# Linear attention and MLP: gamma folded into weights and biases, residual sums taken from PSUM, values copied by ScalarE

## The reference, cut to what matters

```
xn   = rmsnorm(h, scale1)                       # h * scale1 * (sqrt(128) + 1e-6) / norm(h)
q, k, v = xn @ qkv_w.T                          # 16 heads of 8
q, k = exp(-0.5 q^2), exp(-0.5 k^2)
kv   = sum over rows of k (x) v                 # per sequence and head
out  = (q @ kv) / (q @ sum(k) + 1e-6)
h1   = h + gamma * (out @ proj_w.T + proj_b)
hdd  = gelu(rmsnorm(h1, scale2) @ conv1_w.T + conv1_b)      # 256 wide
x    = x + h1 + gamma * (hdd @ conv2_w.T + conv2_b)
```

## Time and profile before

| what | value |
|---|---|
| median of 3 runs | 1204.99 us (1204.27 to 1205.66) |
| the profiled execution | 1205.75 us, of which the span of instructions is 1203.9 us |
| linear stage, 311.7 to 372.2 us | 60.5 us |
| MLP stage, 372.2 to 404.6 us | 32.4 us |
| busy share of the span | PE 86%, DVE 63%, ACT 46%, POOL 37% |

### The profile page before, as it was taken

The page is one execution under the profiler, slowest core; times in us unless marked ns, Lnnn a source line. Parts: engine busy times, 40 slices in busy tenths (PEclk is TensorE's granted clock), DMA queues, the critical chain, the costliest instruction groups (busy, mean ns, idle before and its releaser), DMA issues. The chain is left out here.

```text
span 1203.9 us, 30164 instructions
## 1 busy us (share of the span) xinstructions
PE 1036.5 (86%) x12369; PEld 782.5 (65%) x12369; DVE 753.6 (63%) x1475; ACT 549.6 (46%) x1000; POOL 447.1 (37%) x496
## 2 busy tenths in 40 slices
PE   5899999998576679999999989997889958699992
PEld 4788888886454557777777756665436625567771
DVE  2455655554495568888888858886568778631222
ACT  2455555554233246666666635553545424342220
POOL 1132333322245624444444433321324157236142
PEclk9999999999898769999999979997989869889996
DMA  8300050000000100000000000000784110011324
GB/s 246 127 1 1 2 142 2 1 1 1 0 1 1 36 1 2 3 3 3 2 3 2 2 1 2 2 2 2 228 323 124 30 36 3 3 57 55 97 91 126
DMA packets 37943, 53.15 MB, mean 44 GB/s; under 512 B 3024, under 2 KB 29264, under 8 KB 37424
## 3 DMA queue, kind: packets, MB, share of 16 engines
q1 hardware_dynamic: 35824, 46.97, 12.4%
q0 software_dynamic: 1984, 4.26, 1.0%
HBM read 29.08 MB, written 22.14 MB: 43 GB/s over the span
## 5 line engine op out<-in xcount | busy, mean ns | idle before, releaser
L1515 ACT COPY e_PT<-probsT 128x512 f32<-128x512 f32 x192 | 103.5, 589 | 154.8 <-PE probsT L1363 154.8
L1363 PE MATMUL probsT<-W,e_P 128*128 128x128 f32 x768 | 106.8, 284 | 15.5 <-ACT e_P L1522 15.5
L505 POOL TENSOR_TENSOR c_P<-c_P,c_rl 128x1024 f32<-128x1024 f32 x32 | 60.7, 1896 | 127.7 <-DVE c_rl L645 127.7
L1522 ACT ACTIVATE e_P<-e_P 128x1024 f32<-128x1024 f32 x96 | 102.7, 1070 | 5.6 <-DVE e_P L1620 4.0
L1363 PEld LDWEIGHTS probsT<-W,e_P 128*128 128x128 f32 x768 | 86.8, 144 | 19.1 <-ACT e_P L1522 17.7
L1617 DVE TENSOR_REDUCE e_mx<-scores 128x16 f32<-128x1024 f32 x64 | 78.4, 1225 | 30.6 <-PE scores L1351 29.3
L642 DVE TENSOR_REDUCE c_rl<-c_P 128x8 f32<-128x1024 f32 x32 | 39.0, 1220 | 81.9 <-ACT c_P L329 81.9
L542 PEld LDWEIGHTS misc<-c_xs,c_AQ 128*128 128x128 f32 x488 | 62.2, 194 | 35.0 <-issue 33.4
L1190 POOL TENSOR_TENSOR e_RK<-e_Ks,W 128x512 f32<-128x512 f32 x64 | 65.9, 1039 | 51.2 <-PE scores L1351 28.3
L1620 DVE TENSOR_TENSOR e_P<-scores,e_mx 128x1024 f32<-128x1024 f32 x64 | 78.4, 1225 | 6.5
L1376 PEld LDWEIGHTS mixed<-e_Vbd,e_PT 128*64 128x64 f32 x2048 | 64.9, 138 | 26.1 <-issue 19.3
(11 more groups left out here) (366 smaller groups left out, 2345.7 us busy)
## 6 DMA issues: line engine op xcount, KB each, us to landing
hbm_dist<-u_Z SPq DMA_DIRECT2D x16, 768.0 KB, 8.4
u_S<-hbm_dist SPq DMA_DIRECT2D x64, 128.0 KB, 2.8
e_w<-in_w SPq DMA_DIRECT2D x12, 256.0 KB, 2.8
W<-in_wpack SPq DMA_DIRECT2D x1, 2489.0 KB, 13.1
hbm_slots<-c_blank SPq DMA_DIRECT2D x6, 350.0 KB, 6.2
e_xin<-hbm_slots SPq DMA_DIRECT2D x6, 350.0 KB, 3.4
W<-in_wpack SPq DMA_DIRECT2D x1, 2048.0 KB, 8.7
hbm_results<-c_blank SPq DMA_DIRECT2D x1, 2048.0 KB, 11.5
```

What stands on the lines that cost most here:

```text
L505: pool.tensor_tensor(pr, pr, bc(rl[:, a.up, :].unsqueeze(2), [P, PAIRS, KEYS]), ALU.mult).then_inc(s["scaled"], 1)
L1363: last = pe.transpose(K.psT[:, i * P:(i + 1) * P], Pr[:, n % 2, i * P:(i + 1) * P], K.ident)
L1515: act.copy(PT[:, n % 2, half * 512:(half + 1) * 512], K.psT[:, half * 512:(half + 1) * 512]).then_inc(s["tcopied"], 1)
L1522: act.activation(Pr[:, n % 2, :], Pr[:, n % 2, :], ACT.Exp, scale=0.5 if n < TOTAL else CSCALE).then_inc(s["exped"], 1)
```

## The change

The products with gamma leave the loops. Four operations at the start of `stage_linear` make `projG = projT * gamma`, `projB = proj_b * gamma`, `downB = conv2_b * gamma` and `downG = conv2T * gamma`. PE multiplies by `projG` and `K.downG`, so PSUM already holds gamma times the product. POOL adds the two bias rows to `Xmid` and to `X` in the linear stage, right after a group's `scales`; in the MLP stage it adds `Xmid` to `X` one step earlier than before. DVE, which copied PSUM plus bias into `ya`, now adds PSUM straight into `Xmid` (line 782 of the changed kernel) or `X`; the buffers `ya` are gone. The copy of the values goes from DVE to ACT, and the two masked columns of a tile are made by one operation in place of two.

```diff
@@ stage_linear, DVE
+                def scaled_weights():
+                    gamma = row("gamma")
+                    dve.tensor_tensor(projG[:, :], w("projT"), gamma, ALU.mult).then_inc(s["weights"], 1)
+                    dve.tensor_tensor(projB[:, :], row("proj_b"), gamma, ALU.mult).then_inc(s["weights"], 1)
+                    dve.tensor_tensor(downB[:, :], row("conv2_b"), gamma, ALU.mult).then_inc(s["weights"], 1)
+                    dve.tensor_tensor(K.downG[:, :, :], w("conv2T").rearrange("p (c d) -> p c d", c=2),
+                                      bc(gamma.unsqueeze(1), [P, 2, D]), ALU.mult)
...
-                        for b in range(TB):
-                            last = dve.tensor_scalar(KV[:, a.par, i, b, D:], w("headmask"),
-                                                     ps[:, TB * D + b:TB * D + b + 1], None, ALU.mult)
+                        last = dve.tensor_tensor(KV[:, a.par, i, :, D:], bc(w("headmask").unsqueeze(1), [P, TB, HEADS]),
+                                                 bc(ps[:, TB * D:TB * D + TB].unsqueeze(2), [P, TB, HEADS]), ALU.mult)
...
-                def bias(a):
+                def mid(a):
...
                     dve.wait_ge(s["y"], a.n + 1)
-                    wait(dve, s["xm"], a.n - 1)
-                    dve.tensor_tensor(ya[:, a.par, :, :], pY[:, 0:N].rearrange("p (i d) -> p i d", i=G),
-                                      bc(row("proj_b").unsqueeze(1), [P, G, D]), ALU.add).then_inc(s["ya"], 1)
+                    dve.wait_ge(s["xb"], 2 * (a.n + 1))
+                    xl = K.Xmid[:, a.n * G:(a.n + 1) * G, :]
+                    dve.tensor_tensor(xl, pY[:, 0:N].rearrange("p (i d) -> p i d", i=G), xl, ALU.add).then_inc(s["ya"], 1)
...
                 first = At(0, 0, 1)
                 stats(first)
                 stats(first.plus(1))
+                scaled_weights()
                 xnorm(first)
@@ stage_linear, POOL
-                def mid(a):
+                def biases(a):
...
-                    pool.wait_ge(s["ya"], a.n + 1)
-                    y = ya[:, a.par, :, :]
-                    pool.tensor_tensor(y, y, bc(row("gamma").unsqueeze(1), [P, G, D]), ALU.mult).then_inc(s["yg"], 1)
-                    pool.wait_ge(s["yg"], a.n + 1)
-                    xl = K.Xmid[:, bass.ds(a.n * G, G), :]
-                    pool.tensor_tensor(xl, xl, y, ALU.add).then_inc(s["xm"], 1)
+                    pool.wait_ge(s["xn"], a.n + 1)
+                    for x, v in ((K.Xmid, projB), (K.X, downB)):
+                        xl = x[:, a.n * G:(a.n + 1) * G, :]
+                        pool.tensor_tensor(xl, xl, bc(v[:, :].unsqueeze(1), [P, G, D]), ALU.add).then_inc(s["xb"], 1)
@@ stage_linear, ACT (phi)
-                    act.wait_ge(s["v"], a.n + 1)
+                    act.wait_ge(s["kv"], a.n + 1)
+                    wait(act, s["KV"], a.n - 1)
+                    for b in range(TB):
+                        last = act.copy(vb[64 * b:64 * b + 64, a.par, :, b * D:(b + 1) * D],
+                                        pKV[64 * b:64 * b + 64, :].rearrange("p (i c) -> p i c", i=G)[:, :, D:])
+                    last.then_inc(s["v"], 1)
@@ stage_mlp, DVE (bias becomes result, in the same place of the step)
-                    wait(dve, s["ym"], a.n - 1)
-                    dve.tensor_tensor(ya[:, a.par, :, :], pY[a.par][:, 0:N].rearrange("p (i d) -> p i d", i=G),
-                                      bc(row("conv2_b").unsqueeze(1), [P, G, D]), ALU.add).then_inc(s["ya"], 1)
+                    dve.wait_ge(s["xsum"], a.n + 1)
+                    xl = K.X[:, a.n * G:(a.n + 1) * G, :]
+                    dve.tensor_tensor(xl, pY[a.par][:, 0:N].rearrange("p (i d) -> p i d", i=G), xl, ALU.add).then_inc(s["ya"], 1)
@@ stage_mlp, POOL (residual)
-                    pool.wait_ge(s["ya"], a.n + 1)
...
+                    xl, ml = K.X[:, a.n * G:(a.n + 1) * G, :], K.Xmid[:, a.n * G:(a.n + 1) * G, :]
+                    pool.tensor_tensor(xl, xl, ml, ALU.add).then_inc(s["xsum"], 1)
```

More of the change, by code:

```diff
@@ L681, in stage_linear @@
     K.Xmid = K.early.enter_context(nc.sbuf_tensor("Xmid", [P, TILES, D], F32))
+    K.downG = K.early.enter_context(nc.sbuf_tensor("downG", [P, 2, D], F32))
     with ExitStack() as st:
         s = K.sems(st, "l2_", "weights chain var scaled rs xn turned xnT q kv squared phi v kvm KV num rden rdenok o oT oTc y "
-                              "ya yg xm")
+                              "ya xb")
         sb = lambda n, sh, dt=F32: st.enter_context(nc.sbuf_tensor("l2_" + n, sh, dt))
-        Wqkv = sb("Wqkv", [D, 3 * D])
+        Wqkv, projG = sb("Wqkv", [D, 3 * D]), sb("projG", [D, D])
+        projB, downB = sb("projB", [P, D]), sb("downB", [P, D])
         st6, mv = sb("st6", [P, 2, G, 6]), sb("mv", [P, 2, G, 2])
@@ L788, in step @@
                     xnorm(a.plus(1))
-                    values(a)
                     stats(a.plus(2))
                     divide(a.plus(-1))
-                    bias(a.plus(-2))
+                    mid(a.plus(-2))
                 first = At(0, 0, 1)
@@ L831, in _ @@
                 scales(first.plus(1))
-                run_units(pool, 1, GROUPS, step, 2)
+                pool.wait_ge(s["weights"], 6)
+                run_units(pool, 1, GROUPS, step, 0)
             @block.scalar
@@ L871, in _ @@
                 xT(At(0, 0, 1))
+                act.wait_ge(s["weights"], 3)
                 run_units(act, 1, GROUPS, step, 2)
@@ L946, in step @@
                     proj(a.plus(-2))
-                pe.wait_ge(s["weights"], 3)
                 turn(At(0, 0, 1))
+                pe.wait_ge(s["weights"], 4)
                 run_units(pe, 1, GROUPS, step, 2)
@@ L994, in xnorm, with result @@
                     last.then_inc(s["xn"], 1)
-                def bias(a):
+                def result(a):
                     if not inside(a):
@@ L1006, in step @@
                     squares(a.plus(2))
-                    bias(a.plus(-1))
+                    result(a.plus(-1))
                 first = At(0, 0, 1)
@@ L1028, in residual @@
                         return
-                    pool.wait_ge(s["ya"], a.n + 1)
-                    y = ya[:, a.par, :, :]
-                    at = bass.ds(a.n * G, G)
-                    pool.tensor_tensor(y, y, bc(row("gamma").unsqueeze(1), [P, G, D]), ALU.mult).then_inc(s["yg"], 1)
-                    pool.tensor_tensor(K.X[:, at, :], K.X[:, at, :], K.Xmid[:, at, :], ALU.add).then_inc(s["yg"], 1)
-                    pool.wait_ge(s["yg"], 2 * a.n + 2)
-                    pool.tensor_tensor(K.X[:, at, :], K.X[:, at, :], y, ALU.add).then_inc(s["ym"], 1)
+                    xl, ml = K.X[:, a.n * G:(a.n + 1) * G, :], K.Xmid[:, a.n * G:(a.n + 1) * G, :]
+                    pool.tensor_tensor(xl, xl, ml, ALU.add).then_inc(s["xsum"], 1)
                 def step(a):
                     scales(a.plus(2))
-                    residual(a.plus(-1))
+                    residual(a)
                 first = At(0, 0, 1)
@@ L1097, in down @@
                             last = pe.matmul(pY[a.par][:, i * D:(i + 1) * D], hT[:, a.par, c, i * P:(i + 1) * P],
-                                             w("conv2T", c * P, P), start=(c == 0), stop=(c == 1))
+                                             K.downG[:, c, :], start=(c == 0), stop=(c == 1))
                     last.then_inc(s["y"], 1)
```

19 lines of the change are left out of this document (4 added, 15 removed).

## The result

The changed kernel takes 1187.15 us (median of 6 runs, 1186.93 to 1191.66) against 1205.92 us (median of 6, 1204.27 to 1206.57) of the kernel before. In two later sessions, on two chips, the changed kernel had 1189.99 us against 1205.38, ratio 0.9867 (0.984 to 0.9894), and 1190.19 against 1205.36, ratio 0.9883 (0.9837 to 0.9929). So the gain is real in every session, but both kernels scatter much more than the three runs shown before let me think.

What follows compares the result with a forecast made beforehand. Chains between engines, with no engine full, were taken to bound both stages. Gains of 5.2 + 0.4 + 1.6 + 1.8 + 2.8, less 0.1 for weights, gave 11.7 us: 1204.99 to 1193.3 us, range 1190.5 to 1197.0.

Steps and rivals of the forecast that it cites:

- The period, 5.2 us: Linear stage: time per group falls from 5.97 to 5.13 us, a gain of 5.2 us from first to last sums.
- M: Linear stage: time of the new masking on DVE, forecast 1.08 us against 1.70, with bounds 1.24 and 0.95.
- the path over PE: Linear stage: masking, normalising, hop, then PE's transposes to sums at 1.72 us, and 1.17 to masking; 5.13 us a group.
- The path over ACT, 4.67: Linear stage: chain from sums through qkv products, ACT's copies and exponentials, 4.67 us; shorter than PE's, 0.46 to spare.
- The last masking and the stage's end on VectorE, 0.4 + 1.6: Linear stage's end: the last masking gains 0.4 us; ending with DVE and not POOL gains 1.6.
- The scaled weights, -0.1: Linear stage's start: four products with gamma fit where DVE idles for POOL's first scale; they cost nothing or 0.1 us.
- The MLP stage, 1.8 + 2.8: MLP stage: all eight groups run at 2.59 us, gaining 1.8; ending with DVE and not POOL gains 2.8.
- the term for the clock: MLP stage: the clock's rise can come a little sooner or later, about one more us of spread.
- a rival in which it changes at one place: Attention stage's entry: 2.4 GHz is kept where the clock was 1.2 GHz, worth 6.9 us, total 1186.4; chance 7%.
- Rival 1: Linear stage: POOL's two new additions fall on DVE's normalising, margin 0.17 us; costs 5.7 us, total 1199.0; chance 9%.
- my own list: Signs of being wrong: DVE's normalising starts inside a POOL addition, sums wait for ACT, or the attention stage's clock differs.
- Rivals 2, 4 and 5: MLP loop stays with DVE and POOL, 1194.7, 8%; low clock lasts longer, 1207.4, 3%; nothing arrives, 1205, 3%.

Runs made afterwards that it cites:

- after again: The changed kernel profiled a second time, nothing edited against the changed kernel; the profiled execution took 1187.21 us.

## Why the prediction was wrong, by its own steps

**The mechanisms held, and so did their sum, in part by luck.** 11.7 us were forecast; the two stages give 12.0 us between the first two profiles and 12.3 between the two with equal later stages, and 11.6 are left at equal clock over all runs. In the first pair the linear stage gave 1.6 more than its 7.2 and the MLP stage 1.4 less than its 4.6, and the two errors nearly cancel. Term by term:

- *The period, 5.2 us.* Measured 6.5: the first and the last sums (first pieces) are 325.14 and 358.55, so 33.4 us against 39.9. The period is 4.66, not 5.13. M was 0.87, not 1.08, below its bound of 0.95: a joined masking takes 0.18 us but the next operation starts 0.09 to 0.10 behind it, and I had taken 0.20 from start to start out of the row of 0.19. And the rest of the turn was 3.79, not 4.05, in all three kernels in which the sums no longer wait for ACT (this one and the experiments with the copies alone and with two masks). I had subtracted the wait of 0.22 from the path over PE, but the wait had cost more: it also kept the sums' weights from being loaded ahead. The load's own row in the kernel before shows 0.41 us, not 0.22:

```profile
340.71 0.30 PEld L893 LDWEIGHTS scores<-l_vb,l_phk 128*128 128x128 f32 x2 [0.41 <-ACT l_phk L864]
```

  From the transposes to the sums there were 1.94 us before and 1.56 after, 0.38 less. With the wait, load and product start together (340.71 here, 335.93 with the masks alone) and the first two products take 0.70 us; without it, the load starts 0.11 us sooner (334.55 and 334.66 in "after again") and they take 0.60. Against that, the collision at the end took 0.83 back, which I had as a rival and not as a term.
- *The path over ACT, 4.67, as the shorter one.* It is shorter than 4.67: from the sums (334.53) the last exponential ends 4.50 us later (339.03), and PE starts the next sums 0.16 after that. So some 0.16 us are to spare, where I counted 0.46.
- *The last masking and the stage's end on VectorE, 0.4 + 1.6.* From the last sums to the next stage 8.64 us before (363.63 to 372.27), 6.46 after: 2.2.
- *The scaled weights, -0.1.* Nothing. The rule from the Trainium skill ("SBUF — State Buffer", "Who interferes with whom"), by which they could cost 1.04 us, did not show in these rows: four operations with two SBUF inputs ran beside POOL's root at 0.26 to 0.41 us. With POOL's 128x256 additions the rule does agree in the kernel before: VectorE's squares in the MLP stage, which read one tile as both inputs, took 0.80 us beside such an addition (389.31) and 0.28 free. Normalising, with one such input, was held by them as well.
- *The MLP stage, 1.8 + 2.8.* 3.2 in the first pair of profiles, 4.6 in the second. In the first, 0.9 was lost because the second product came 10.4 us after the stage's start against 9.5 before, its rows still at the 1.2 GHz level, and 0.4 in the gap to the next stage.

**The step that failed is the term for the clock, and with it the range.** I gave the clock "about one more" microsecond of spread, for its rise in the MLP stage, and nothing for the stages that nobody edited; a rival in which it changes at one place had 7%. Its size is 10 us: one kernel's runs go from 1198.6 to 1208.6, and unedited stages from 426.3 to 432.1 us. Over all runs the changed kernel has 11.0 us less at 1.2 GHz, worth 3.9 us, a term that my sum puts at nothing; with it, and with that scatter, the range would have had to reach below 1187. That the three runs shown lay within 1.4 us said nothing on it. The rival named the attention stage's entry, and there I had the wrong event: the changed kernel's entry is still at 0.50 and its clock rises 34.8 us after the stage's start where it was 36.6; what differs is the sum of such stretches over the whole rest of the program. So 1187 lies near the rival's 1186.4 by another way than the rival's. Where the matmuls kept the clock up at the entry, it was worth 4.3 us there, not 6.9.

**The other rivals.** Rival 1, POOL on the normalising, happened at the last normalising of every profile of the changed kernel and in the last four turns with the masks alone. In the steady turn of the changed kernel POOL's second addition ends at 336.69, later than I had it, and the normalising begins at 336.47, a sign of being wrong by my own list, but it isn't held. The turn before it with the 0.54 us says why:

```profile
331.34 0.73 POOL L819 TENSOR_TENSOR X<-X,l_downB 128x256 f32<-128x256 f32 x1
331.61 0.54 DVE L739 TENSOR_SCALAR Xmid<-X,l_mv,l_rs 128x128 f32<-128x128 f32 x1
```

It began 0.27 us into the addition and ended 0.81 after the addition's start. In nine profiles of this case 63 others began from 0.03 us before to 0.13 behind the start of an addition and ended 0.80 to 0.89 after it; 26 began 0.51 or more into one, and none was held. Less the 0.33 that a free one takes, the hold ends about 0.5 us into an addition that the trace shows at 0.73; that is an estimate from these rows. The steady normalising begins 0.51 into it. So the rival missed by a few hundredths of a microsecond, not by the 0.17 that I had. Rivals 2, 4 and 5 did not happen.

**What stays open.** Why executions of one kernel differ in the clock, and by which rule a shift of 1.6 us moves a kernel from one set of lengths to another, is not settled; the one shift that moved the time is shown, four offsets are too few for a curve.

## What to carry to other kernels

When a short path stops a second one from starting, take its wait off the second path and also what that wait kept from being prepared; three kernels with the same remainder (3.79 us here) are a better price than a difference read off one trace. An engine's busy time can hold another's work: 5.5 us of VectorE's in the MLP stage went without one of its instructions changing in number. Judge an edit of a few microseconds by the stages that it touches, from two executions whose other stages have the same length, since unedited stages moved by 5 us with the clock. Where a stage begins with TensorE waiting and the granted clock at 0.5, matmuls that nobody reads in those waits can shorten it, by 4.3 us here; count what they delay against it, 2.1 us here.

## What the runs showed of the hardware

- One stage with the same instructions has few lengths, not a continuum: in the 13 profiles without matmuls added, the attention stage took 426.3 to 426.5, 429.4 to 430.3 or 431.8 to 432.1 us, with 51, 57 or 63 us at 1.2 GHz. The kernel before and its variants had all three, and so had the changed one and its.
- A delay of 1.6 us ahead of it cost 5.6 us in the mean, in one of four kernels with such delays.
- A VectorE normalising of 128x128 that met a POOL addition of 128x256 ended 0.80 to 0.89 us after the addition's start, whether it began with it or 0.27 us into it (64 cases in nine profiles); begun 0.51 us or more into it, it took at most its free 0.34 (26 cases).
- After a VectorE operation of 128x32 out of PSUM the next one started 0.09 to 0.10 us behind it, though it is shown at 0.18; pairs of 128x16 with a scalar operand took 0.28 free and up to 0.83 beside a POOL addition of 128x256, while the joined form was not held by an addition of the same shape (0.18 at 335.94, beside POOL's at 335.96).
